# Moving the first batch's query evacuation, GpSimd's conv taps and the second batch's projections in the head of a fused AdaLN, attention and MoE kernel

## The reference, cut to what matters

```
Q, K, V = y @ Wq.T + bq, y @ Wk.T + bk, y @ Wv.T + bv        # 16 heads of 8
scores  = einsum('bhqd,bhkd->bhqk', Q, K) / sqrt(8)
scores  = conv1d over k, 3 taps, mixing the 16 heads, + conv_b
out     = softmax(scores) @ V @ Wo.T + bo ;  x = x + out
x       = x + moe_top1(lora_linear(x))
```

## Time and profile before

| what | value |
|---|---|
| median of 3 runs | 233.69 us |
| profiled execution, its own time | 232.46 us |
| its span in the trace | 230.6 us |
| TensorE matmul busy | 219.9 us, 95% |
| TensorE weight loads busy | 178.8 us, 78% |
| VectorE busy | 189.7 us, 82% |
| GpSimd busy | 166.2 us, 72% |
| ScalarE busy | 164.2 us, 71% |
| granted TensorE clock, mean | 0.995 of full |

### The profile page before, as it was taken

One profiled execution on the slowest core, in us unless ns is written; L12 is line 12 of the kernel. 1 busy time (PEld: TensorE's weight loads), 2 busy tenths in 40 slices (PEclk: granted clock), 3 DMA queues, 4 the chain that ended last, 5 costly groups with the idle time before them and its releaser, 6 DMA issues.

```text
span 230.6 us, 5463 instructions
## 1 busy us (share of the span) xinstructions
PE 219.9 (95%) x1741; PEld 178.8 (78%) x1741; DVE 189.7 (82%) x484; ACT 164.2 (71%) x296; POOL 166.2 (72%) x193
## 2 busy tenths in 40 slices
PE   8999998799999999999999999999999999999990
PEld 8445786487888788888878887888788898989980
DVE  2469999989898998999799799979979777793460
ACT  2455598899698988889798898989898681205310
POOL 1019988799979989898988889898982704361785
PEclk9999999999999999999999999999999999999997
DMA  6993004537727463565556365474546540930233
GB/s 207 349 440 120 3 1 153 121 141 169 209 83 204 154 136 139 134 208 132 154 191 136 144 138 189 102 220 150 134 167 139 187 89 21 347 91 3 23 34 34
DMA packets 16117, 33.42 MB, mean 145 GB/s; under 512 B 1618, under 2 KB 12882, under 8 KB 15826
## 3 DMA queue, kind: packets, MB, share of 16 engines
q1 hardware_dynamic: 14514, 31.94, 46.6%
q0 software_dynamic: 1152, 0.52, 2.6%
q10 hardware_dynamic: 432, 0.71, 0.9%
HBM read 20.32 MB, written 13.37 MB: 146 GB/s over the span
## 4 chain that ended last, share of the span: by engine, by line
PE 85%; DVE 5%; DMA 4%; issue 2%; POOLq 1%; POOL 1%; ACT 1%; SPq 1%; DVEq 0%
PE tp L1107 13%; PE sc L955 13%; PE sc L957 11%; PE sc L956 11%; PE pvbank L975 6%; PE pvbank L973 5%; PE tp L1241 3%; PE sc L1219 3%; PE sc L877 2%; PE misc L1002 2%; DMA PT<-swap 2%; DMA swap<-w2s 2%; PE sc L1168 2%; PE sc L1171 2%; PE sc L896 2%
## 5 line engine op out<-in xcount | busy, mean ns | idle before, releaser
L424 ACT ACTIVATE Pb<-Pb,nbias 128x512 f32<-128x512 f32 x128 | 90.2, 719 | 20.0 <-DVE Pb L639 18.6
L639 DVE TENSOR_SCALAR_CACHE_REDUCE Pb<-sc,col 128x512 f32<-128x512 f32 x128 | 91.5, 732 | 10.6 <-PE sc L957 10.4
L955 PE MATMUL sc<-Kh,Ql 128*128 128x512 f32 x124 | 56.5, 456 | 2.1 <-POOL Kl L272 1.3
L957 PE MATMUL sc<-Kh,Qh 128*128 128x512 f32 x124 | 48.9, 395 | 0.0
L956 PE MATMUL sc<-Kl,Qh 128*128 128x512 f32 x124 | 48.7, 393 | 0.0
L1107 PEld LDWEIGHTS tp<-cst,Pb 128*128 128x128 f32 x316 | 38.9, 140 | 11.6 <-ACT PT L469 1.4
L1107 PE MATMUL tp<-cst,Pb 128*128 128x128 f32 x316 | 47.4, 272 | 0.2 <-ACT PT L469 0.2
L469 ACT ACTIVATE PT<-tp 128x512 f32<-128x512 f32 x77 | 44.8, 581 | 1.0 <-PE tp L1107 0.5
L284 POOL TENSOR_TENSOR td<-ta,tc_ 128x512 f32<-128x512 f32 x31 | 43.1, 1390 | 2.6
L272 POOL TENSOR_TENSOR Kl<-kc,Kh 128x512 fp32r<-128x512 f32 x28 | 36.1, 1289 | 10.2 <-ACT Kh L419 9.0
L778 DVE STREAM_TRANSPOSE w2s<-Pb 128x512 f32<-128x512 f32 x45 | 31.6, 703 | 0.0
(11 more groups left out here) (230 smaller groups left out, 297.9 us busy)
## 6 DMA issues: line engine op xcount, KB each, us to landing
swap<-w2s SPq DMA_DIRECT2D x15, 768.0 KB, 3.3
PT<-swap SPq DMA_DIRECT2D x60, 192.0 KB, 3.8
w1s<-in_w SPq DMA_DIRECT2D x1, 2048.0 KB, 9.6
w2s<-in_w SPq DMA_DIRECT2D x1, 2048.0 KB, 7.8
cst<-in_consts SPq DMA_DIRECT2D x1, 652.0 KB, 5.1
xTs<-in_xT SPq DMA_DIRECT2D x2, 256.0 KB, 3.1
we<-in_wexp SPq DMA_DIRECT2D x2, 256.0 KB, 3.4
b2s<-in_b2row SPq DMA_DIRECT2D x1, 512.0 KB, 10.4
```

The source lines that it names most:

```text
L424: act.activation(Pb[:, k, :], Pb[:, k, :], ACT.Exp, bias=nbias[:, k:k + 1], scale=-1.0)\
L639: dve.tensor_scalar(Pb[:, k, :], SC[k % 4][:, :], cb, None, ALU.subtract, ALU.min, accum_out=nbias[:, k:k + 1]).then_inc(s["mx"], 1)
L955: pe.matmul(SC[k][:, :], ql, Kh[:, h2, :], start=True, stop=False)
L957: pe.matmul(SC[k][:, :], qh, Kh[:, h2, :], start=False, stop=True).then_inc(s["sc"], 1)
```

## The change

Six moves, and one small addition:

1. The copy of the first batch's queries out of their bank goes from VectorE (`queries(0)` in `first_head`) to ScalarE, as scale times input plus bias; a VectorE instruction on one column (`bqs`) makes the bias. ScalarE waits for its own copy (`qev`) before `high_queries(0)`.
2. GpSimd's `outer_taps(1)` waits for `kc` to reach 1, the first head's smoothed keys; `bbr` goes from in front of the taps to behind `outer_taps(3)`.
3. ScalarE's `high_first(0)` goes ahead of `y(1)`; `high_first(1)` goes behind `exp(0)`, `keys(1)` behind `exp(1)`, `wz` behind `exp(3)`.
4. TensorE's `wtm` matmuls go from in front of `gated(0)` to behind `project_keys(0)`; VectorE's `wte` addition goes behind `hidden_front(1, 0)`.
5. `project_keys(1)` goes from in front of the first scores to behind the second unit's; `wzm` goes behind the fourth unit's.
6. `project_queries(1)` goes from in front of the first group to in front of its unit 4, `project_values(1)` to in front of its unit 6.

```
@@ gpsimd @@
             fetch_taps(1, 1, 1)
-            pool.wait_ge(s["ones"], 1)
-            pool.wait_ge(s["wte"], 1)
-            pool.tensor_scalar(bbr, ones[:, :], col[:, BB:BB + 1], 1.0, ALU.mult, ALU.mult).then_inc(s["bbb"], 1)
             pool.wait_ge(s["cw"], 1)
             pool.wait_ge(s["kev"], 1)
+            pool.wait_ge(s["kc"], 1)
             outer_taps(1, 0, 1)
...
             outer_taps(3, 0, 1)
+            pool.wait_ge(s["ones"], 1)
+            pool.wait_ge(s["wte"], 1)
+            pool.tensor_scalar(bbr, ones[:, :], col[:, BB:BB + 1], 1.0, ALU.mult, ALU.mult).then_inc(s["bbb"], 1)
@@ scalar @@
+            act.wait_ge(s["qmm"], 1)
+            act.wait_ge(s["bqs"], 1)
+            act.activation(q32[0][:, :], FRONT[0][2][:, :], ACT.Identity, bias=bqs[:, 0:1], scale=-float(DH) ** -0.5)\
+                .then_inc(s["qev"], 1)
+            act.wait_ge(s["qev"], 1)
             high_queries(0)
+            high_first(0)
             y(1)
-            high_first(0)
-            keys(1)
-            act.wait_ge(s["wzm"], 1)
-            act.activation(wz[:, :, :].rearrange("p b m -> p (b m)"), PV[:, 0:B * W], ACT.Copy).then_inc(s["wze"], 1)
-            high_first(1)
...
-            for k in range(AHEAD):
-                exp(k, k)
+            exp(0, 0)
+            high_first(1)
+            exp(1, 1)
+            keys(1)
+            exp(2, 2)
+            exp(3, 3)
+            act.wait_ge(s["wzm"], 1)
+            act.activation(wz[:, :, :].rearrange("p b m -> p (b m)"), PV[:, 0:B * W], ACT.Copy).then_inc(s["wze"], 1)
             high_half(2, 0)
@@ vector @@
+            dve.tensor_scalar(bqs[:, :], col[:, BQ:BQ + 1], -float(DH) ** -0.5, None, ALU.mult).then_inc(s["bqs"], 1)
...
+            hidden_front(1, 0)
             dve.wait_ge(s["wtm"], 1)
             dve.tensor_tensor(weffT, MISC[:, B * C:2 * B * C].rearrange("p (b c) -> p b c", b=B),
                               lo_w[:, 3:4, :].broadcast_to([128, B, C]), ALU.add).then_inc(s["wte"], 1)
-            hidden_front(1, 0)
...
                 hidden_front(1, 1)
-                queries(0)
@@ tensor @@
             first_layer(1, 1)
+            gated(0)
+            first_layer(1, 2)
+            pe.wait_ge(s["wq"], 16)
+            project_keys(0)
             pe.wait_ge(s["wefe"], B)
             for b in range(B):
                 mm = pe.matmul(MISC[:, (B + b) * C:(B + b + 1) * C], bs[:, b, :], lo_w[:, 0, :], start=True, stop=True)
             mm.then_inc(s["wtm"], 1)
-            gated(0)
-            first_layer(1, 2)
-            pe.wait_ge(s["wq"], 16)
-            project_keys(0)
             first_layer(1, 3)
...
             project_values(0)
-            project_keys(1)
-            pe.matmul(PV[:, 0:B * W], wq[:, 4, :], weff[:, :, :].rearrange("p b m -> p (b m)"), start=True, stop=True)\
-                .then_inc(s["wzm"], 1)
...
                 pe.matmul(SC[k][:, :], qh, Kh[:, 0, :], start=False, stop=True).then_inc(s["sc"], 1)
+                if k == 1:
+                    project_keys(1)
+            pe.matmul(PV[:, 0:B * W], wq[:, 4, :], weff[:, :, :].rearrange("p b m -> p (b m)"), start=True, stop=True)\
+                .then_inc(s["wzm"], 1)
-            pe.wait_ge(s["wze"], 1)
-            project_queries(1)
-            project_values(1)
...
             for u in range(TURN):
+                if u == 4:
+                    pe.wait_ge(s["wze"], 1)
+                    project_queries(1)
+                elif u == 6:
+                    project_values(1)
                 unit(0, 0, u)
```

More of the change, by code:

```diff
@@ L120, in build @@
         spare = sb("spare", [128, 4])
+        bqs = sb("bqs", [128, 1])
         nbias = sb("nbias", [128, RING])
@@ L174, in build @@
             slt gm wtm wte lam lae wzm wze bbb xbo xtk xto disp0 disp1 dsp dtea dted onr k0 kl0 b2g hm0 hmm heva hevd hevx eom
-            dump shr pay hot tok six eog add""".split()
+            dump shr pay hot tok six eog add bqs""".split()
         s = {n: sem("s_" + n) for n in names}
```

## The result

The changed kernel takes 235.12 us in the median of 20 executions (234.14 to 237.45), the kernel before 234.03 in the median of 20 beside it (233.01 to 235.42). The ratio is 1.005 with a 95% interval of 1.003 to 1.0071: **1.2 us slower (0.7 to 1.7)**. The forecast was +1.5. The profiled execution has a span of 233.2 us for 230.6, and 2.6 us is more than the medians differ by. The execution profiled before was a favourable one (232.46 us against 234.03), so the traces are compared stretch by stretch, not by their ends.

The account below looks back on a forecast made before the run. VectorE was taken to set the first group's pace, TensorE the steady stage after it. 0.74 for GpSimd's late sum and 0.73 for ScalarE's late Kh, taken as +1.5 on 233.69, gave 235.2 us; range 233.4 to 236.6.

Parts of the forecast that it names:

- its two terms: On VectorE: first maximum 0.74 us later through GpSimd's late sum, plus 0.73 us standing still for ScalarE's Kh of head 1.
- Part 1: TensorE's small matmuls: first_layer(1, 3) waits for the moved wtm, starting about 0.67 us later; VectorE's last hidden_front +0.48.
- Parts 2 and 3: First head's keys: kc ends 1.08 us earlier, at 19.81; ScalarE's queries copy takes 0.69 us, Kh ends at 20.74.
- Part 4: GpSimd starts late and takes turns with VectorE: first sum ends at 23.63, first maximum starts at 24.95, +0.74 us.
- The turns: VectorE and GpSimd at SBUF: whoever comes second waits out the first; +1.5 with turns, +0.6 without.
- Part 5: New wait: VectorE's Kl of head 1 stands still about 0.73 us for ScalarE's Kh, now queued behind exp(0).
- Part 6: TensorE's moved projections cost nothing in the group and gain nothing in the head: 3.1 us of cover against 1.75.
- Part 7: Later heads' keys: GpSimd's Kl of head 4 comes 2.7 us later, at 43.9; the end still moves by +1.5.
- the case: Rival: GpSimd takes over as the bound, its +2.7 us not absorbed; 236.4 us, chance 0.15.
- The advice that the prediction names: On the shared SBUF port: schedule around whichever engine is on the critical path, so holding GpSimd back is right for kc.

Follow-up runs that it names:

- e8: Changed kernel with the wtm matmuls and the wte addition moved back in front of gated(0): 234.18 us, ratio 1.0032 to the kernel before.
- e1: Changed kernel without GpSimd's wait for the first head's smoothed keys: 234.51 us, ratio 1.0042 to the kernel before.
- e9: Changed kernel with VectorE's values copy and first maximum put ahead of middle_tap(1), filling its wait for GpSimd: 235.4 us, ratio 1.0071.
- e2: Changed kernel with ScalarE's copy of head 1's keys ahead of exp(0): 234.27 us, ratio 1.004 to the kernel before.
- e6: Kernel before with only ScalarE's copy of head 1's keys put behind exp(0): 233.17 us, ratio 1.0001.
- e7: Changed kernel with the second batch's keys, queries, values and wz back where the kernel before has them: 235.43 us, ratio 1.0069.
- e11: e10 without GpSimd's wait for the first head's smoothed keys: 233.97 us, ratio 1.0011 to the kernel before.
- e3: Changed kernel with both the edits of e1 and e2: 233.83 us, ratio 1.001 to the kernel before.
- e4: Kernel before with only GpSimd's wait for the first head's smoothed keys added: 233.96 us, ratio 1.0027.
- e10: e9 with the wtm matmuls and the wte addition moved back in front of gated(0): 235.05 us, ratio 1.0084 to the kernel before.
- e12: Kernel before with both batches' queries copied by ScalarE and nothing else: 232.66 us, ratio 0.9965.
- e5: Kernel before with only the first batch's queries copy on ScalarE: 233.0 us, ratio 1.0002.

## Why the prediction was right, and where it wasn't

**Size and sign**: +1.5 forecast, +1.2 measured (0.7 to 1.7). At the first outputs, where the prediction also says +1.5, the trace shows +0.86. The other 0.3 us of the medians is placed nowhere. The sum came out near in part by luck, since one of its two terms is nearly nothing and the other isn't what decides. TensorE's wait before head 4's scores was to grow; it went from 1.34 to 1.38 us.

**Part 1, right.** `first_layer(1, 3)` starts at 16.17, which is 0.69 us later behind the first matmul (0.67 forecast), `hidden_front` 0.60 (0.48). e8 shows that it passes to the last turn in full, 0.59 us: the gate hangs GpSimd's start on it. Without the gate most of it is hidden: e1 has the late `hidden_front` too, and its last turn is 0.22 us behind the kernel before. (The terms as written add up to 0.71; the prediction says 0.67.)

**Parts 2 and 3, right.** `kc` ends at 19.61 (19.81 forecast), ScalarE's copy takes 0.68 us (0.69), `Kh` of head 0 ends at 20.54 (20.74). These times are of a trace that began 0.35 us early: counted from the first matmul, each comes 0.15 us later than forecast.

**Part 4, right in place, near in size, wrong in what it decides.** GpSimd's sum ends at 23.50 (23.63), the first maximum starts at 24.82 (24.95); counted from the first matmul the maximum is +0.96 and not +0.74. The turns weren't strict: `Kl` of head 0 was served ahead of `tc_` and ended at 21.66 (22.41), and the first scores started at 21.80 (22.55). That left the end of the sum where it was. But the delay on VectorE is not the price: e9 takes 2 us out of VectorE's path and the last turn doesn't move.

**Part 5, the term that failed.** The idle is there (0.64 for 0.73), but it costs 0.13 us at the last turn, not 0.73 (e2 and e6), and nothing that the medians show: alone in e6 the next collision falls away, and in e2 a collision takes its place. The prediction has a collision add 0.3 to it. An idle gap in front of an instruction that would wait for the port anyway is no cost.

**Part 6, right.** From the first maximum to the last turn e7 takes 21.78 us, the changed kernel 21.78.

**Part 7, the mechanism that I underrated.** GpSimd's `Kl` of head 4 ended at 42.85 (43.9 forecast), 1.7 us late by the clock and 2.05 counted from the first matmul, instead of 2.7. It caught up more because it had idled more than the 0.35 us that I read: 0.77 us ahead of head 2 as well. I took GpSimd's lateness as absorbed and gave the case 0.15 with +2.7. e9 to e11 show that it does bind, from head 2 on, while the price at the last turn is 0.7 with Part 1 in it. VectorE's path is nearly as long: the last turn stands at 39.76 to 39.98 us in the kernel before, e1, e3, e6 and e11, where VectorE sets it, and at 39.88 to 40.10 in e4, e8 and e10, which have the gate without the late wtm and where GpSimd sets it. So cutting either alone gains little.

**Not foreseen:** that the kernel's end depends on when a transfer lands. TensorE's wait before the second outputs was 0.35 us in the one trace I had and 0.40 to 1.35 in the thirteen others. Every delay of the last turn starts that round trip later.

**Left open:** the medians follow the marks only roughly. e1 and e10 are 1.0 and 2.0 us slower than the kernel before by their ratios, with last turns 0.22 and 0.20 us later.

The Trainium skill ("SBUF — State Buffer", "Who interferes with whom") says that whichever engine issues first has the shared port for its whole instruction and the other is blocked. The trace agrees: e2's `Kl` ended 0.6 us behind the end of GpSimd's sum. The advice that the prediction names with it stands in the same page's summary. Here it did not pay. The gate takes 0.9 us of collision off `kc`, but e1, without the gate, meets GpSimd's sum one instruction earlier and still has its first maximum 1.16 us sooner than the changed kernel, and the engine that was held back became the bound.

## What to carry to other kernels

The length of an idle gap isn't its price. If the instruction behind the gap would have waited for something else anyway, such as a shared port, little is won by closing the gap, so close or fill it in an experiment before giving it a price. Where one engine feeds another over a chain of many short steps (here GpSimd's `outer_taps`, 3.0 to 3.7 us for each head), a late start need not be made up at the first consumer that happens to have slack; follow it to the last one. Before holding an engine back, look at how long it idles: a start that is later by more than it idles can make it the bound (here 3.3 us later, with 1.1 us of idle ahead of the two `Kl`). And take work off the engine that has none to spare without adding a wait in front of it: that alone (e12) gained, while reordering the head for the same end lost.

## What the runs showed that I had not expected

- Turns at the port aren't repeatable. `kc` of head 0, with the same program in front of it, took 1.65 us in e5 and 0.98 in e12, and the first maximum came 0.60 us earlier in e12.
- The steady stage repeats closely: the third interval between outputs was 9.84 to 9.87 us in all fourteen traces. What varies between executions lies in good part at the transfers: TensorE's wait at the first group alone was 0.35 to 1.35 us.
- A transfer of the same blocks (`swap<-w2s`) took 4.20 us in the execution profiled before, 5.23 in that of the changed kernel and 4.85 in that of e5. What makes it longer I did not test.
